# Runs of edges per target tile: ten partitions and three small matmuls in place of one partition, in a two-layer graph kernel

## The chip, the cores and the metric

The kernel runs on one core of one Trainium2 chip. The metric is the device time of one execution in microseconds, the median of three runs. A core has TensorE (matmuls and transposes into PSUM), VectorE, ScalarE, GpSimd, and SyncE, which issues most transfers. Each engine works through its own instructions in program order; engines are tied to each other only by semaphores.

## What is computed

Two graph attention networks with a layer norm behind each, on 1250 nodes of 768 features and 20000 edges sorted by target (self loops are added). The edges do not enter the kernel's later stages one by one: the first stage turns them into a matrix of counts C[dst, src], and the attention is then dense work on it. Of the reference, what the first stage needs:

```python
loops = jnp.arange(N)
src = jnp.concatenate([edge_index[0], loops])
dst = jnp.concatenate([edge_index[1], loops])
x1 = jax.nn.relu(x @ W_ah + b_ah)
# in every attention layer, per edge:
e = leaky_relu(as_n[src] + ad_n[dst], 0.2)
p = exp(e - segment_max(e, dst)[dst])
out = segment_sum(p / segment_sum(p, dst)[dst] * h[src], dst)
```

## The kernel before, in words

`gnn_two_layers` calls one stage after another (`counts_and_x1`, `project`, `aggregate_layer0` and so on). Each stage ends with a barrier of all engines, so a stage begins when the one before is over. The change lies in the first stage, `counts_and_x1`, alone.

**What the stage makes.** The counts of edges for ten tiles of 125 target nodes (T = 125, NT = 10), a mask from them, and x1 = relu(x W + b) transposed, for five blocks of 250 nodes (NB = 5). Products in float32 precision are made of a high and a low part of each operand (`w_hi`, `w_lo`, `xT_hi`, `xT_lo`).

**How edges are counted.** The 20000 edges lie on 40 partitions (ER = 40), 500 on each, and an edge run is one such partition; four steps (RUN = 4) of 125 edges make a run. VectorE casts them to float (L216) and takes least and greatest target of each run (L217, L218). TensorE turns edges and ends (L365, L368): the ends come out on all 128 partitions, 40 columns of least and 40 of greatest, in bank 1 of `p_turn`. Because edges are sorted, a target tile meets a contiguous range of runs. The kernel finds for every tile the first run, the number of runs and how many were handled before: `range_i[0, 0..2, tile]`. Before, VectorE does this on one partition with 10 x 40 = 400 elements (L222 to L241), in buffers that lie in the count matrix `CT`, and a scan makes the running sum. Every `step(...)` is an instruction that signals, and a wait for it (`Chain`).

**The loops over runs.** `one_hots(t)` on VectorE reads three values of `range_i` into registers and loops over the runs; for each of four steps it waits for a free buffer (`hot_free`), writes `src_hot` (125 x 1250, L254) and `dst_hot` (125 x 125, L255). `count(t)` on TensorE reads two values, opens the banks with three band matmuls (the self loops, L382) and adds `dst_hot` times `src_hot`, three matmuls a step (L388). Four buffers lie between the two.

**The order written out by hand.** VectorE: the ranges, `rest_of_x(0, 0)` (L269), then per block one_hots, two rest_of_x, score weights (L502), mask (L260), rest_of_x1, one_hots and so on. TensorE: turn the edges, wait for the constants and for `ranges_ready` (L373, L374), turn x (0, 0) and (0, 1) (L417), then per block count, turn_x, x1 products (L431), turn_row and so on. ScalarE rounds x (L322), stages the count rows (L309) and keeps turned rows. GpSimd: iotas and constants (L191 to L200), six tiles of W split into two parts (L204, L206; a copy `w_hi` and a difference `w_lo`), then the DMA issues of the score weights (L484, L488), each of which waits, from the fourth on, for VectorE's use. SyncE: edges, x, bias, then the six tiles of W, of which tile k waits until tile k - 2 is split (L182).

Of the kernel before, what the change touches and what calls it, by code (L numbers as in the profile page):

```python
# [101 lines left out]
def counts_and_x1(nc, core, src, dst, x, w_ah, b_ah, w_gat, a_gat):  # L102
# [4 lines left out]
    with ExitStack() as ctx:  # L107
        sb, pb, sem = core.tools(ctx)
        dst_ends = sb("dst_ends", [ER, 2], F32)
        ends_row = sb("ends_row", [128, 2, ER], F32)  # L110
        edge_col = sb("edge_col", [T, 2, RUN, 2 * ER], F32)

        spare = CT[0:1, :, :].rearrange("p t n -> p (t n)")[:, 0:2 * 5 * NT * ER].bitcast(F32) \
            .rearrange("p (a t e) -> p a t e", a=5, t=NT)
        meets, meets_b, meets_c = (spare[:, i] for i in range(3))
        tile_lo, run_no = (spare[:, i].bitcast(I32) for i in (3, 4))
        range_f = sb("range_f", [1, 3, NT], F32)
        ones_row = sb("ones_row", [1, NT], F32)
# [32 lines left out]
        ranges_ready = sem("ranges_ready")  # L151
        hot_ready = sem("hot_ready")
# [37 lines left out]
        def _(pool):  # L190
            pool.iota(node_no[:], [[1, N]], base=0, channel_multiplier=0).then_inc(consts, 1)  # L191
            pool.iota(tile_lo, [[T, NT], [0, ER]], base=0, channel_multiplier=0).then_inc(consts, 1)
            pool.iota(run_no, [[0, NT], [1, ER]], base=0, channel_multiplier=0).then_inc(consts, 1)
# [18 lines left out]
        def _(dve):  # L212
# [9 lines left out]
            step(v.tensor_copy(ends_row[:], p_turn[:, 1, 0:2 * ER].rearrange("p (a c) -> p a c", a=2)))  # L222
            dve.wait_ge(consts, 3)
            least = ends_row[0:1, 0:1, :].broadcast_to([1, NT, ER])
            most = ends_row[0:1, 1:2, :].broadcast_to([1, NT, ER])

            step(v.tensor_tensor(meets, most, tile_lo, ALU.is_ge))
            step(v.scalar_tensor_tensor(meets_b, tile_lo, float(T), least, ALU.add, ALU.is_gt))
            step(v.tensor_tensor(meets, meets, meets_b, ALU.mult))
            step(v.scalar_tensor_tensor(meets_b, run_no, float(-ER), meets, ALU.add, ALU.mult))  # L230
            step(v.scalar_tensor_tensor(meets_c, run_no, 1.0, meets, ALU.add, ALU.mult))
            step(v.tensor_reduce(out=range_f[:, 0, :], in_=meets_b, axis=AX.X, op=ALU.min))
            step(v.tensor_reduce(out=range_f[:, 1, :], in_=meets_c, axis=AX.X, op=ALU.max))
# [126 lines left out]
        def _(pe):  # L360
# [10 lines left out]
            nc.tensor.sem_inc(hot_free, RUN)  # L371
            nc.tensor.sem_inc(row_turned, 1)
            pe.wait_ge(consts, 8)  # L373
            pe.wait_ge(ranges_ready, 1)  # L374
            nc.tensor.sem_inc(ct_done, 1)

            def count(t):
# [1759 lines left out]
```

## Time and profile before

| | us |
|---|---|
| median of 3 runs | 2097.6 |
| lowest and highest | 2096.47, 2100.13 |
| the profiled execution | 2099.49 |
| its span, first to last instruction | 2097.7 |

| engine | busy us | share of the span | instructions |
|---|---|---|---|
| TensorE, matmuls | 1865.0 | 89% | 11272 |
| VectorE | 1492.5 | 71% | 2490 |
| ScalarE | 974.5 | 46% | 1463 |
| GpSimd | 166.1 | 8% | 139 |

TensorE's granted clock over the execution is 0.949 of full speed. The first stage ends near 262 us. In the rows, a time line gives the start in us, the duration in us (of several merged instructions, from the first to the last), the engine, line, operation, output and inputs by the program's names, shapes and count, and in square brackets the idle time in front of it and what ended it. DVE is VectorE, ACT ScalarE, POOL GpSimd, PE TensorE's matmuls, PEld its weight loads. Buffers that lie in others go by the outer one's name: `edge_i` is `x_f`, `edge_f` is `count_row`, `w_raw` is `G`. Durations on GpSimd are rough.

### The profile page before, as it was taken

The page shows a single profiled execution, that of the slowest core. Times are in us where ns is not written, and L with a number is a line of the kernel's source. Part 1 is how long each engine was busy: PE and PEld are TensorE (multiplying, and loading weights), DVE is VectorE, ACT ScalarE, POOL GpSimd, SP SyncE. Part 2 cuts the span into 40 slices and gives each one's busy share as a digit, 9 for nine tenths or more (in the row PEclk, how much of TensorE's full clock was granted, in tenths as well). Part 3 has the DMA queues.
Part 4 walks back from the last instruction along what each step waited for, and adds up shares of the span by engine and source line. Part 5 has one row for each costly group of instructions (what it writes and reads, how often), then busy time and mean ns, then how long its engine had stood idle before and what let it go on. Part 6 is the DMA issues. An engine that isn't in the chain of part 4 may idle for free. (4 is left out here: it accounts for less than half of the span.)

```text
span 2097.7 us, 29944 instructions
## 1 busy us (share of the span) xinstructions
PE 1865.0 (89%) x11272; PEld 1774.4 (85%) x11272; DVE 1492.5 (71%) x2490; ACT 974.5 (46%) x1463; POOL 166.1 (8%) x139
## 2 busy tenths in 40 slices
PE   5998899994999999994989889979999996999888
PEld 4666689994999999994989779978999995999888
DVE  7887759996888888862556619717888885235776
ACT  1222222215687897763222322217888885232433
POOL 5010022100000000000001012100000000000210
PEclk9999999996999999996999889989999998999999
DMA  3111154335243424307856445544423404644402
GB/s 115 49 53 49 38 157 147 104 87 137 65 130 95 108 87 123 89 13 219 236 138 184 137 149 151 169 129 131 143 82 106 139 34 132 176 108 131 116 1 74
DMA packets 203354, 237.69 MB, mean 113 GB/s; under 512 B 98741, under 2 KB 177677, under 8 KB 203224
## 3 DMA queue, kind: packets, MB, share of 16 engines
q1 hardware_dynamic: 195240, 208.32, 34.5%
q0 software_dynamic: 7216, 24.91, 4.0%
q10 hardware_dynamic: 768, 2.70, 0.4%
q8 instruction: 85, 1.39, 0.3%
q14 instruction: 45, 0.37, 0.1%
HBM read 173.99 MB, written 61.90 MB: 112 GB/s over the span
## 5 line engine op out<-in xcount | busy, mean ns | idle before, releaser
L946 PE MATMUL p_o<-h_in,p 125*125 125x193 f32 x2400 | 405.5, 332 | 41.5 <-DVE p L905 20.9
L946 PEld LDWEIGHTS p_o<-h_in,p 125*125 125x125 f32 x2400 | 399.3, 191 | 44.8 <-issue 23.7
L866 ACT ACTIVATE e<-uv,col 125x1250 f32<-125x1250 f32 x240 | 298.5, 1358 | 16.0 <-DMA uv<-uv_rows 14.9
L1404 PE MATMUL p_o<-p_hi,h_parts 125*128 125x416 f32 (+1 forms) x960 | 282.8, 355 | 24.7 <-DVE p_lo L1338 18.4
L1686 PE MATMUL p_y<-fw_hi,f_hi 128*125 128x384 f32 (+1 forms) x680 | 237.9, 350 | 60.7 <-DVE f_lo L1562 58.6
L1686 PE MATMUL p_y<-fw_lo,f_hi 128*125 128x384 f32 (+1 forms) x680 | 235.3, 346 | 0.0
L1686 PE MATMUL p_y<-fw_hi,f_lo 128*125 128x384 f32 (+1 forms) x680 | 234.6, 345 | 0.0
L1562 DVE TENSOR_TENSOR f_lo<-f_raw,f_hi 128x1125 fp32r<-128x1125 f32 (+1 forms) x80 | 101.1, 1265 | 173.6 <-ACT f_hi L1660 173.5
L900 DVE TENSOR_TENSOR e<-e 125x1250 f32<-125x1250 f32 x120 | 174.1, 1451 | 67.5 <-ACT e L866 67.4
L1404 PEld LDWEIGHTS p_o<-p_hi,h_parts 125*128 125x128 f32 x960 | 181.7, 189 | 30.8 <-issue 18.6
L1660 ACT ACTIVATE f_hi<-f_raw 128x1125 fp32r<-128x1125 f32 (+1 forms) x80 | 87.4, 1093 | 251.3 <-PE p_y L1686 215.3
L646 DVE CUSTOM_DVE_ANT_0 max_junk<-src_row,G 125x1250 bf16<-125x1250 f32 x120 | 180.9, 1581 | 9.3 <-DMA src_row<-score_rows 8.6
L733 PE MATMUL p_h<-pw_hi,x1T 128*125 128x384 f32 x720 | 186.2, 340 | 0.0
L1686 PEld LDWEIGHTS p_y<-fw_hi,f_hi 128*125 128x125 f32 x680 | 130.5, 192 | 64.9 <-issue 62.0
L905 DVE SCALAR_TENSOR_TENSOR p<-e,CT 125x1250 f32<-125x1250 f32 x120 | 175.3, 1461 | 5.7 <-PE p_o L946 1.7
L1146 PE MATMUL p_h<-pw_hi,x2T 128*125 128x256 f32 x960 | 173.7, 284 | 0.0
L1404 PE MATMUL p_o<-p_lo,h_parts 125*128 125x416 f32 (+1 forms) x480 | 169.9, 354 | 0.0
L1146 PEld LDWEIGHTS p_h<-pw_hi,x2T 128*125 128x125 f32 x960 | 148.4, 188 | 0.0
L388 PE MATMUL p_count<-src_hot,dst_hot 125*125 125x416 bf16 (+1 forms) x588 | 126.6, 372 | 18.9 <-DVE dst_hot L255 18.9
L1296 ACT ACTIVATE e<-uv,col 125x416 f32<-125x416 f32 (+1 forms) x240 | 139.6, 630 | 0.0
L1146 PE MATMUL p_h<-pw_lo,x2T 128*125 128x256 f32 x480 | 136.1, 284 | 0.0
L388 PEld LDWEIGHTS p_count<-src_hot,dst_hot 125*125 125x125 bf16 x588 | 73.8, 145 | 72.1 <-DVE dst_hot L255 55.4
(227 smaller groups left out, 3259.4 us busy)
## 6 DMA issues: line engine op xcount, KB each, us to landing
f_raw<-turned SPq DMA_DIRECT2D x40, 562.5 KB, 4.3
f_raw<-turned SPq DMA_DIRECT2D x40, 500.0 KB
h_rows<-h_out SPq DMA_DIRECT2D x32, 560.0 KB
h_parts<-h_rows SPq DMA_DIRECT2D x40, 448.0 KB
uv<-uv_rows SPq DMA_DIRECT2D x24, 546.9 KB
turned<-out_f SPq DMA_DIRECT2D x18, 625.0 KB
h_rows<-h_out SPq DMA_DIRECT2D x24, 424.4 KB
h_in<-h_rows SPq DMA_DIRECT2D x24, 424.4 KB
```

The source lines that it names most:

```text
L388: last = nc.tensor.matmul(p_count[:, i, 0:w], dst_hot[:, h, :], src_hot[:, h, a:a + w], start=False, stop=False, skip_group_check=True)
L646: v.tensor_tensor_reduce(out=junk[:, t % 2, :], in0=src_row[:, h % 2, :], in1=G[:, t, :], scale=1.0, scalar=NO_EDGE, op0=ALU.add, op1=ALU.max,
L733: last = nc.tensor.matmul(p_h[:, (u * NT + t) % 4, 0:width], xp[:, k, at], wp[:, u, k, :], start=(k == 0 and n == 0), stop=(k == KD - 1 an ...
L866: last = a.activation(e[:, g % RING, kind, :], uv[:, hh, kind, :], ACT.Exp, bias=col_src[kind][:, bass.ds(i * 2 + hh, 1), s])
L900: v.tensor_tensor(e[:, g % RING, 0, :], e[:, g % RING, 0, :], e[:, g % RING, 1, :], ALU.max).then_inc(more_ready, 1)
L905: v.scalar_tensor_tensor(p[:, g % RING, :], e[:, g % RING, 0, :], 1.0, CT[:, s, :], ALU.min, ALU.mult).then_inc(p_ready, 1)
L946: last = nc.tensor.matmul(p_o[:, b, n * 256:n * 256 + C0 + 1], p[:, g % RING, d * T:(d + 1) * T], h_in[:, hh, s, 0:C0 + 1], start=(s == 0 ...
L1146: last = nc.tensor.matmul(p_h[:, n % 4, 0:HALF1], xp[:, k, at], wp[:, q % 2, k, :], start=(k == 0 and j == 0), stop=(k == KD - 1 and j == 2))
L1296: last = a.activation(e[:, g % RING, kind, 0:w], uv[:, i % 2, kind, at:at + w], ACT.Exp, bias=col_src[kind][:, i, s:s + 1])
L1404: last = nc.tensor.matmul(p_o[:, bank(n, c), 0:w], h[:, s, kind, cols].bitcast(F32R), pp[:, g % RING, 0:w], start=(s == 0 and j == 0), sto ...
L1562: v.tensor_tensor(f_lo[:, kh], f_raw[:, kh], f_hi[:, kh].bitcast(F32), ALU.subtract).then_inc(f_lo_done, 1)
L1686: last = nc.tensor.matmul(p_y[:, t % 2, 0:CW + extra], fp[:, kh, kk, :], wp[:, k, :], start=(k == 0 and n == 0), stop=(k == K - 1 and n == 2))
```

## The change

The ranges are found with the ten tiles on ten partitions: each instruction then has 40 elements or one a partition, and the ends are read where TensorE put them, in PSUM, where every partition has them. The tile's first node comes from an iota over partitions. First run and count stand as two columns of `range_f` [10, 4]. TensorE brings them to one partition: two matmuls with the identity turn them, and one with `later` (1 where the column's tile is later than the row's) gives the sum of the counts of all tiles before, so the scan goes. VectorE casts the result from bank 2 of `p_turn` (L241's successor). GpSimd makes `later` with a memset, a wait and a select, ahead of its other constants. On TensorE the three matmuls stand behind a wait for `ranges_found`; the waits for the constants and for `ranges_ready` move behind `turn_x(0, 0)` and `turn_x(0, 1)`. Nothing else changes.

```diff
--- before.py
+++ after.py
@@ -107,15 +107,14 @@
     with ExitStack() as ctx:
         sb, pb, sem = core.tools(ctx)
         dst_ends = sb("dst_ends", [ER, 2], F32)
-        ends_row = sb("ends_row", [128, 2, ER], F32)
         edge_col = sb("edge_col", [T, 2, RUN, 2 * ER], F32)
 
-        spare = CT[0:1, :, :].rearrange("p t n -> p (t n)")[:, 0:2 * 5 * NT * ER].bitcast(F32) \
-            .rearrange("p (a t e) -> p a t e", a=5, t=NT)
-        meets, meets_b, meets_c = (spare[:, i] for i in range(3))
-        tile_lo, run_no = (spare[:, i].bitcast(I32) for i in (3, 4))
-        range_f = sb("range_f", [1, 3, NT], F32)
-        ones_row = sb("ones_row", [1, NT], F32)
+        tile_lo = sb("tile_lo", [NT, 2], F32)
+        tile_lo_i = sb("tile_lo_i", [NT, 1], I32)
+        run_no_i = sb("run_no_i", [NT, ER], I32)
+        meets = sb("meets", [NT, 3, ER], F32)
+        range_f = sb("range_f", [NT, 4], F32)
+        later = sb("later_tiles", [NT, NT], F32)
         range_i = sb("range_i", [1, 3, NT], I32)
         node_no = sb("node_no", [T, N], I16)
         src_hot = sb("src_hot", [T, RUN, N], BF16)
@@ -149,6 +148,9 @@
         edges_turned = sem("edges_turned")
         cols_ready = sem("cols_ready")
         ranges_ready = sem("ranges_ready")
+        later_ready = sem("later_ready")
+        ranges_found = sem("ranges_found")
+        ranges_turned = sem("ranges_turned")
         hot_ready = sem("hot_ready")
         hot_free = sem("hot_free")
         counted = sem("counted")
@@ -189,8 +191,12 @@
         @block.gpsimd
         def _(pool):
             pool.iota(node_no[:], [[1, N]], base=0, channel_multiplier=0).then_inc(consts, 1)
-            pool.iota(tile_lo, [[T, NT], [0, ER]], base=0, channel_multiplier=0).then_inc(consts, 1)
-            pool.iota(run_no, [[0, NT], [1, ER]], base=0, channel_multiplier=0).then_inc(consts, 1)
+            pool.iota(tile_lo_i[:], [[0, 1]], base=0, channel_multiplier=T).then_inc(consts, 1)
+            pool.iota(run_no_i[:], [[1, ER]], base=0, channel_multiplier=0).then_inc(consts, 1)
+            pool.memset(later[:], 1.0).then_inc(later_ready, 1)
+            pool.wait_ge(later_ready, 1)
+            pool.affine_select(out=later[:], in_=later[:], compare_op=ALU.is_gt, fill=0.0, base=0,
+                               pattern=[[1, NT]], channel_multiplier=-1).then_inc(later_ready, 1)
             for m in (band, ident_b, zeros_b):
                 pool.memset(m[:], 0.0).then_inc(consts, 1)
             pool.wait_ge(consts, 6)
@@ -219,26 +225,20 @@
             dve.wait_ge(edges_turned, 1)
             v.tensor_copy(edge_col[:, :, :, 0:ER],
                           p_turn[0:T, 0, 0:2 * RUN * ER].rearrange("p (a b c) -> p a b c", a=2, b=RUN)).then_inc(cols_ready, 1)
-            step(v.tensor_copy(ends_row[:], p_turn[:, 1, 0:2 * ER].rearrange("p (a c) -> p a c", a=2)))
             dve.wait_ge(consts, 3)
-            least = ends_row[0:1, 0:1, :].broadcast_to([1, NT, ER])
-            most = ends_row[0:1, 1:2, :].broadcast_to([1, NT, ER])
-
-            step(v.tensor_tensor(meets, most, tile_lo, ALU.is_ge))
-            step(v.scalar_tensor_tensor(meets_b, tile_lo, float(T), least, ALU.add, ALU.is_gt))
-            step(v.tensor_tensor(meets, meets, meets_b, ALU.mult))
-            step(v.scalar_tensor_tensor(meets_b, run_no, float(-ER), meets, ALU.add, ALU.mult))
-            step(v.scalar_tensor_tensor(meets_c, run_no, 1.0, meets, ALU.add, ALU.mult))
-            step(v.tensor_reduce(out=range_f[:, 0, :], in_=meets_b, axis=AX.X, op=ALU.min))
-            step(v.tensor_reduce(out=range_f[:, 1, :], in_=meets_c, axis=AX.X, op=ALU.max))
-            step(v.tensor_scalar(range_f[:, 0, :], range_f[:, 0, :], float(ER), float(ER - 1), ALU.add, ALU.min))
-            step(v.tensor_tensor(range_f[:, 1, :], range_f[:, 1, :], range_f[:, 0, :], ALU.subtract))
-            step(v.tensor_scalar(range_f[:, 1, :], range_f[:, 1, :], 1.0, None, ALU.max))
-            step(v.memset(ones_row[:], 1.0))
-
-            step(v.tensor_tensor_scan(range_f[:, 2, :], ones_row[:], range_f[:, 1, :], 0.0, ALU.mult, ALU.add))
-            step(v.tensor_tensor(range_f[:, 2, :], range_f[:, 2, :], range_f[:, 1, :], ALU.subtract))
-            v.tensor_copy(range_i[:], range_f[:]).then_inc(ranges_ready, 1)
+            step(v.tensor_copy(tile_lo[:, 0:1], tile_lo_i[:]))
+            step(v.tensor_scalar(tile_lo[:, 1:2], tile_lo[:, 0:1], float(T), None, ALU.add))
+            least, most = (p_turn[0:NT, 1, a * ER:(a + 1) * ER] for a in range(2))
+            step(v.tensor_scalar(meets[:, 0, :], most, tile_lo[:, 0:1], None, ALU.is_ge))
+            step(v.scalar_tensor_tensor(meets[:, 0, :], least, tile_lo[:, 1:2], meets[:, 0, :], ALU.is_lt, ALU.mult))
+            step(v.scalar_tensor_tensor(meets[:, 1, :], run_no_i[:], float(-ER), meets[:, 0, :], ALU.add, ALU.mult))
+            step(v.scalar_tensor_tensor(meets[:, 2, :], run_no_i[:], 1.0, meets[:, 0, :], ALU.add, ALU.mult))
+            step(v.tensor_reduce(out=range_f[:, 2:3], in_=meets[:, 1, :], axis=AX.X, op=ALU.min))
+            step(v.tensor_reduce(out=range_f[:, 3:4], in_=meets[:, 2, :], axis=AX.X, op=ALU.max))
+            step(v.tensor_scalar(range_f[:, 0:1], range_f[:, 2:3], float(ER), float(ER - 1), ALU.add, ALU.min))
+            v.tensor_scalar(range_f[:, 1:2], range_f[:, 3:4], range_f[:, 0:1], 1.0, ALU.subtract, ALU.max).then_inc(ranges_found, 1)
+            dve.wait_ge(ranges_turned, 1)
+            v.tensor_copy(range_i[:], p_turn[0:1, 2, 0:3 * NT].rearrange("p (a n) -> p a n", a=3)).then_inc(ranges_ready, 1)
             dve.wait_ge(ranges_ready, 1)
             dve.wait_ge(cols_ready, 1)
 
@@ -368,10 +368,13 @@
                 last = nc.tensor.transpose(p_turn[:, 1, a * ER:(a + 1) * ER],
                                            dst_ends[:, a:a + 1].broadcast_to([ER, 128]), ident[0:ER, 0:ER])
             last.then_inc(edges_turned, 1)
+            pe.wait_ge(later_ready, 2)
+            pe.wait_ge(ranges_found, 1)
+            for a in range(2):
+                nc.tensor.matmul(p_turn[0:1, 2, a * NT:(a + 1) * NT], range_f[:, a:a + 1], ident[0:NT, 0:NT], start=True, stop=True)
+            nc.tensor.matmul(p_turn[0:1, 2, 2 * NT:3 * NT], range_f[:, 1:2], later[:], start=True, stop=True).then_inc(ranges_turned, 1)
             nc.tensor.sem_inc(hot_free, RUN)
             nc.tensor.sem_inc(row_turned, 1)
-            pe.wait_ge(consts, 8)
-            pe.wait_ge(ranges_ready, 1)
             nc.tensor.sem_inc(ct_done, 1)
 
             def count(t):
@@ -437,6 +440,8 @@
 
             turn_x(0, 0)
             turn_x(0, 1)
+            pe.wait_ge(consts, 8)
+            pe.wait_ge(ranges_ready, 1)
             for b in range(NB):
                 count(2 * b)
                 turn_x(b, 2)
```

## Rows read from the trace of the kernel before

**Rows 1.** The page, part 1: engine, busy us, share of the span, instructions.
```profile
PE 1865.0 (89%) x11272; PEld 1774.4 (85%) x11272; DVE 1492.5 (71%) x2490; ACT 974.5 (46%) x1463; POOL 166.1 (8%) x139
```

**Rows 2.** Busy time of each engine by window of 10 us.
```profile
core 0: us, PE busy (x) PEld busy (x) DVE busy (x) ACT busy (x) POOL busy (x), PEclk, DMA share, GB/s
...
10.00:20.00 10.00, 0.00 (x0) 0.00 (x0) 9.72 (x10) 0.00 (x0) 9.50 (x7) 1.00 0.36 118
...
40.00:50.00 10.00, 9.19 (x76) 8.51 (x74) 6.61 (x31) 4.61 (x10) 2.15 (x4) 1.00 0.61 178
```

**Rows 3.** Timeline of VectorE, 9 to 42 us: start, duration, line.
```profile
9.87 0.49 DVE L220 COPY edge_col<-p_turn 125x320 f32<-125x320 f32 x1 [2.34 <-PE p_turn L368]
...
10.55 1.26 DVE L227 TENSOR_TENSOR CT<-ends_row,CT 1x400 f32<-1x400 f32 x1
...
12.95 1.80 DVE L229 TENSOR_TENSOR CT<-CT 1x400 f32<-1x400 f32 x1
...
18.32 0.56 DVE L233 TENSOR_REDUCE range_f<-CT 1x10 f32<-1x400 f32 x1
18.91 1.12 DVE L234 TENSOR_SCALAR range_f<-range_f 1x10 f32<-1x10 f32 x1
...
21.16 1.47 DVE L239 TENSOR_TENSOR_SCAN range_f<-ones_row,range_f 1x10 f32<-1x10 f32 x1
...
22.86 0.17 DVE L241 CAST range_i<-range_f 1x30 int32<-1x30 f32 x1
...
28.82 0.55 DVE L254 TENSOR_SCALAR src_hot<-node_no,edge_col 125x1250 bf16<-125x1250 int16 x1 [1.85 <-issue]
...
30.07 0.54 DVE L254 TENSOR_SCALAR src_hot<-node_no,edge_col 125x1250 bf16<-125x1250 int16 x1
...
39.22 0.67 DVE L269 TENSOR_TENSOR xT_lo<-p_x,xT_hi 128x500 fp32r<-128x500 f32 x1
...
41.85 0.35 DVE L502 CUSTOM_DVE_ANT_0 wa_by_junk<-wa_by_w,wa_by_a 128x192 bf16<-128x192 f32 x1
```

**Rows 4.** Timeline of GpSimd, 3 to 26 us.
```profile
3.10 0.48 POOL L193 IOTA CT<- 1x400 int32 x1
...
9.84 1.54 POOL L206 TENSOR_TENSOR w_lo<-G,w_hi 128x768 fp32r<-128x768 f32 x1
11.32 1.17 POOL L204 CAST w_hi<-G 128x768 fp32r<-128x768 f32 x1
12.57 1.75 POOL L206 TENSOR_TENSOR w_lo<-G,w_hi 128x768 fp32r<-128x768 f32 x1
14.58 0.86 POOL L204 CAST w_hi<-G 128x768 fp32r<-128x768 f32 x1 [0.26 <-DMA G<-in_w_ah]
...
18.46 1.54 POOL L206 TENSOR_TENSOR w_lo<-G,w_hi 128x768 fp32r<-128x768 f32 x1
...
23.86 1.54 POOL L206 TENSOR_TENSOR w_lo<-G,w_hi 128x768 fp32r<-128x768 f32 x1
25.34 0.71 POOL L484 DMA_DIRECT2D wa_by_a<-in_a_gat  x1
```

**Rows 5.** Timeline of TensorE and ScalarE at the first tiles of x.
```profile
23.13 1.90 PE L417 MATMUL p_x<-ident,x_in 125*128 125x125 f32 x8 [13.37 <-issue]
24.28 1.28 ACT L322 ACT_TABLE_LOAD   x1 [24.28 <-PE p_x L417]
```

**Rows 6.** Timeline near 92 us; landing times of line L488's 36 issues.
```profile
91.69 1.14 POOL L484 DMA_DIRECT2D wa_by_a<-in_a_gat  x1
91.90 0.81 DVE L260 TENSOR_SCALAR G<-count_row 125x1250 bf16<-125x1250 f32 x1
...
DMA to landing us min/median/max: 2.5/2.8/4.4
```

**Rows 7.** TensorE's groups, 29.5 to 32.9 us, then 33.2 to 39.3 us: busy, mean ns.
```profile
L388 PE MATMUL p_count<-src_hot,dst_hot 125*125 125x416 bf16 (+1 forms) x11 | 3.6, 510 | 3.5 <-DVE dst_hot L255 3.5
...
L388 PE MATMUL p_count<-src_hot,dst_hot 125*125 125x416 bf16 (+1 forms) x35 | 6.6, 344 | 0.0
```

## The prediction, made before the change was run

> **What bounds the kernel now.** The page first: TensorE is busy for 89% of the span [rows 1], and the chain that the page follows back from the last instruction stays in the last stage, so it says nothing of the first. What is done at the start is worth its time only if everything behind it moves up. So I read the windows of the first 30 us next: from 10 to 20 us TensorE does nothing while VectorE is busy for 9.72 and GpSimd for 9.50 of 10 us [rows 2]. Then the timeline by engine. VectorE's copy of the turned edges starts at 9.87, and a chain of fourteen small instructions follows, on one partition, each waiting for the one before, up to the cast at 22.86 to 23.03 [rows 3]. TensorE stands in front of `ranges_ready` and turns x only at 23.13 [rows 5]; ScalarE loads a table and rounds, VectorE forms the rest and reads three registers, and the first one-hot starts at 28.82 [rows 3, 5]. Every later step of the stage waits for counts, and counts wait for one-hots. No transfer with a time of its own stands behind this. So the quantity to forecast is **when the one-hots of tile 0 are through**: now at 39.22, where VectorE goes on to L269 [rows 3].
>
> **Why the chain takes 12.5 us.** The arithmetic is small, but its durations are not its own. L229 runs 12.95 to 14.75, and GpSimd's w_lo of 12.57 to 14.32 ends 0.43 before it; L239 (10 elements) runs 21.16 to 22.63 and L234 (10 elements) 18.91 to 20.03, GpSimd's instruction beside L234 ending at 20.00 [rows 3, 4]. L227 is held the same way to 11.38 and then needs 0.43. Not held: L233, a reduction that begins 0.14 before GpSimd's instruction of 18.46 and runs on beside it for 0.42 us, and L220, which reads PSUM and lies wholly beside GpSimd's w_lo of 9.84 to 11.38 [rows 3, 4]. So VectorE's SBUF-to-SBUF forms and GpSimd's instructions exclude each other. They alternate: at 11.38 VectorE, which had waited, went first, and GpSimd's cast of 11.32 took 1.17 in place of 0.86 [rows 4].
>
> **GpSimd's side of it.** It splits six tiles of W, 0.86 and 1.54 us each, with gaps for the loads (0.26 before 14.58), and ends at 25.40; then come its four DMA issues [rows 4]. The change hardly touches this: two iotas of 400 elements (0.48 each) go; two small iotas, a memset, an own wait and a 10x10 select come. Small ones step by about 0.1, the wait and the select by 0.3 each, in all about 0.9 against 0.96, so at most 0.3 either way. That passes to GpSimd's end and to the result at up to one for one. The load of tile k starts when tile k-2 is split, so GpSimd's end is held near 25 by its own work and the round trips of its loads, whether VectorE is quick or not.
>
> **Part by part: the ranges.** Removed: L222 (0.2) and all of L227 to L240. Added on VectorE, after the copy that ends at 10.36: ten small instructions and a cast, and between them three matmuls. My walk, with GpSimd's instructions at 0.86 and 1.54 where they are not held:
> - tile_lo's cast and the add of T read and write SBUF. One element a partition is not in the trace; from below each costs 0.15 (a free small instruction), from above it is held as L234 was. I take held, because L234 is the nearest row: to 11.42, then behind GpSimd's cast to 12.25.
> - Two comparisons that read PSUM: free as L220, 0.2 each, to 12.7.
> - Two products with both inputs in SBUF, 40 elements: the first is held by w_lo to about 13.95, the second falls in GpSimd's wait for its load, 14.1.
> - Two reductions as L233 but with 40 elements, to 14.45; two more small instructions on [10,1], the last behind GpSimd's cast of 14.58, to 15.45.
> So `ranges_found` comes at 15.5; at 13.1 if one-element instructions are never held. TensorE's three matmuls and the semaphores: eight transposes took 1.90 [rows 5], 0.24 each, so 0.7, and x is turned from 16.2. VectorE's cast of the turned ranges lies beside that.
>
> **The x tiles.** The transposes of x wait for nothing that the ranges give, but in program order they stand behind the three matmuls, so the move hides only the last cast. From TensorE's first transpose of x to the first one-hot it is 5.69 now (23.13 to 28.82: transposes, table, rounding, rest, register reads [rows 3, 5]) and nothing in it changes. First one-hot: 16.2 + 5.7 = **21.9**, 6.9 us earlier. With 13.1 it is 19.5.
>
> **What is late next.** At 21.9 GpSimd still has the rest of one w_lo, a cast and a w_lo to do. Now the one-hots start 3.4 us after GpSimd is through and never meet it; no row shows L254 beside a GpSimd computation. It runs SBUF to SBUF with one tensor input, as L234 does, so I take it as held: first one-hot behind the w_lo of 20.85 (to 22.4), done 22.9; its small partner behind the cast, 23.9; the second behind the last w_lo (to 25.45), its partner done at 26.05. Then fourteen steps are left. A step is 0.62 (two from 28.82 to 30.07), sixteen of them took 10.40 (28.82 to 39.22), that is 9.9 and 0.5 in which TensorE, slow at first, held the ring of four buffers. End: 26.05 + 14 x 0.62 + 0.5 = 35.2, against 39.22: **4.0 us**. From 19.5 the same walk gets three steps through before GpSimd ends and gives 34.7, 4.5 us. So about 5 of the gained microseconds meet GpSimd's, and what is saved hardly depends on how long the range chain gets. The 0.5 for the slow TensorE may be spent already beside GpSimd, which lifts 4.0 to 4.5 too. I take **4.3**.
>
> **The DMA issues behind it.** GpSimd's four issues for the score weights, now at 25.34 to 27.64 on an idle VectorE, come under full one-hots. L484 at 91.69 took 1.14 where it took 0.71 at 25.34, and ended 0.12 after L260, beside which it lay [rows 4, 6]. So an issue waits for one VectorE instruction: four of at most 1.2 us end by 30.5, and with 4.4 to landing, the longest [rows 6], the weights are there at 35; L502 wants them at about 37.8 (now 41.85, and 4.0 less [rows 3]). Covered, with 2.8 us to spare; without it each microsecond is lost. The Trainium skill (SBUF — State Buffer, "A bandwidth-pool intuition that's wrong") states a harsher case: a software-generated DMA of about 620 ns took 3100 ns beside a VectorE copy. By that, four issues would end at about 38 and the weights land at 42; no row of this case shows more than the 1.14.
>
> **The sum.** 4.3 us off everything behind it, as the stages follow each other by barriers. The profiled execution's 2099.49 (span 2097.7) becomes 2095.2; it lies 1.9 above the median 2097.6, from which I forecast 2093.3.
>
> **Rivals.**
> - *No exclusion for one-hots* (10%): the whole gain stays, 6.9 (21.9 + 10.4 = 32.3) to 9.3 us with the shorter chain: 2088.3 to 2090.7. For it: nothing but the missing row. Against: L234.
> - *GpSimd is starved* (12%): back-to-back one-hots don't let it in. They end at 32.3, the last split at 35.3, the second DMA issue at 36.5 lands at 40.9, and L502 starts there in place of 41.85: 1 us saved, 2096.6. Against: at 11.38 the one that waited went before the back-to-back one. The skill's figure above would give the same time.
> - *The chain isn't short* (5%): all eight small steps that are no reductions are held, by 1.3 each (the mean of GpSimd's cast and w_lo, with a gap). Then it comes at 20.8, the first one-hot at 27.2, the end at 37.6: 1.6 us saved, 2096.0. The change then fails to do what it says.
> - *Slower, through TensorE's clock* (5%): in the 3.4 us after 29.5 the count's matmuls took 510 ns on the mean, later 344 [rows 7], with TensorE 13 us idle not long before. Fed with a step each 1.6 us beside GpSimd, it may stay at 1.2 GHz until the count is over. Eleven matmuls took 3.6 us, so a step of three costs 0.98, and fourteen from 26.05 end at 39.8: 0.6 late. If the level holds on through the x1 products (76 matmuls in 9.2 us at the high one [rows 2]) up to 8 us more are lost: 2098.2 to 2106, 2102 in the middle. It decides from the point where the level rises only after 33 us.
>
> **How the numbers follow.** My case has 68% and gives 2092 to 2094.8 with the median's own scatter of a microsecond; it is 2093.3. The range: 2089.8 to 2096.8 takes in the starved and the long chain and part of the first rival, and leaves out its lower end and the slow one. A measurement can tell about 0.2%, 4.2 us, from no change, and my forecast lies on that line: half of my case (34%) and the first rival are faster by more, with a part for unknowns 47%; the other half and the two small gains make 47% within; slower 6%.
>
> **What would show it.** In the changed profile: ranges cast done at 14 to 17 us; the first one-hot at 19.5 to 22.5; L254 instances of 1 us and more while GpSimd splits, and GpSimd's w_lo of 1.9 to 2.1; the last w_lo ending at 25 to 26.5; GpSimd's DMA issues at 0.6 to 1.2; L502 not waiting for them; and L269 of group 1 near 35. One-hots of 0.55 beside GpSimd's work would make the first rival true; a wait of L502 for wa_by_w the second. I am wrong by more than 2 us if a later stage has a wait that gives the time back, or if TensorE's granted clock, 0.949 on the mean, shifts by a thousandth or two.

## The result, and the profile after

The changed kernel takes 2089.24 us (median of 7 runs, 2084.95 to 2095.25) against 2098.65 for the kernel before (7 runs, 2092.54 to 2101.0): a ratio of 0.9963, 95% interval 0.9946 to 0.9981. It is faster, by 4 to 11 us. The forecast was 2093.3, in a range of 2089.8 to 2096.8, made on a median of 2097.6 for the kernel before; by the ratio that is 2089.8 (0.9963 x 2097.6), at the very edge of the range (the median itself, 2089.24, lies 0.6 below it), and the direction was right. Two executions, of 6058 and 7938 us, both of the kernel before, are left out of every mean and median below. The profiled execution took 2089.24, its span is 2087.5.

The chain of ranges on VectorE, whose counterpart is [rows 3] (start, duration, line, operation, output and inputs, shapes):

```profile
9.84 0.49 DVE L226 COPY edge_col<-p_turn 125x320 f32<-125x320 f32 x1 [2.35 <-PE p_turn L368]
10.25 0.13 DVE L229 CAST tile_lo<-tile_lo_i 10x1 f32<-10x1 int32 x1
10.41 0.14 DVE L230 TENSOR_SCALAR tile_lo<-tile_lo 10x1 f32<-10x1 f32 x1
...
11.16 0.84 DVE L234 SCALAR_TENSOR_TENSOR meets<-run_no_i,meets 10x40 f32<-10x40 int32 x1
12.03 0.19 DVE L235 SCALAR_TENSOR_TENSOR meets<-run_no_i,meets 10x40 f32<-10x40 int32 x1
...
12.86 0.20 DVE L239 TENSOR_SCALAR range_f<-range_f 10x1 f32<-10x1 f32 x1
13.54 0.18 DVE L241 CAST range_i<-p_turn 1x30 int32<-1x30 f32 x1 [0.48 <-PE p_turn L375]
```

The ranges are ready at 13.72 in place of 23.03. Of the ten small instructions one is held, L234, until GpSimd's cast of 11.12 is over. The one-hots that follow, on the same engine:

```profile
19.34 0.55 DVE L254 TENSOR_SCALAR src_hot<-node_no,edge_col 125x1250 bf16<-125x1250 int16 x1 [1.82 <-issue]
19.81 0.25 DVE L255 TENSOR_SCALAR dst_hot<-node_no,edge_col 125x125 bf16<-125x125 int16 x1
19.97 1.17 DVE L254 TENSOR_SCALAR src_hot<-node_no,edge_col 125x1250 bf16<-125x1250 int16 x1
21.06 1.53 DVE L255 TENSOR_SCALAR dst_hot<-node_no,edge_col 125x125 bf16<-125x125 int16 x1
22.51 1.14 DVE L254 TENSOR_SCALAR src_hot<-node_no,edge_col 125x1250 bf16<-125x1250 int16 x1
23.57 1.53 DVE L255 TENSOR_SCALAR dst_hot<-node_no,edge_col 125x125 bf16<-125x125 int16 x1
25.02 0.53 DVE L254 TENSOR_SCALAR src_hot<-node_no,edge_col 125x1250 bf16<-125x1250 int16 x1
...
34.32 0.67 DVE L269 TENSOR_TENSOR xT_lo<-p_x,xT_hi 128x500 fp32r<-128x500 f32 x1
```

And GpSimd beside them, whose counterpart is [rows 4]:

```profile
17.66 1.55 POOL L212 TENSOR_TENSOR w_lo<-G,w_hi 128x768 fp32r<-128x768 f32 x1
19.98 0.82 POOL L210 CAST w_hi<-G 128x768 fp32r<-128x768 f32 x1 [0.77 <-DMA G<-in_w_ah]
20.88 1.66 POOL L212 TENSOR_TENSOR w_lo<-G,w_hi 128x768 fp32r<-128x768 f32 x1
22.48 0.82 POOL L210 CAST w_hi<-G 128x768 fp32r<-128x768 f32 x1
23.39 1.66 POOL L212 TENSOR_TENSOR w_lo<-G,w_hi 128x768 fp32r<-128x768 f32 x1
24.99 0.71 POOL L489 DMA_DIRECT2D wa_by_a<-in_a_gat  x1
```

The first one-hot starts 9.5 us earlier (19.34 for 28.82), but `dst_hot`, a quarter of a microsecond by itself, takes 1.53 twice: each time GpSimd's w_lo began 0.18 before it, and it ends 0.05 after that w_lo. From 19.97 to 25.02 two steps get done where eight would have. Tile 0's one-hots are through at 34.32 in place of 39.22: of 9.5 us, 4.9 arrive. From 25.02, when GpSimd is done with W, every instruction has its plain length again; what then still stretches some steps is the ring of four buffers, while TensorE is slow.

The remaining 4.3 us of the shorter first stage came after tile 0, in code that the change doesn't touch. Of the windows below, the first two are of before, the third of the changed kernel (after the busy times stand the granted clock, the share of DMA and GB/s):

```profile
190.00:200.00 10.00, 6.70 (x23) 4.30 (x23) 8.18 (x27) 0.91 (x3) 0.55 (x1) 0.66 0.07 22
40.00:250.00 210.00, 193.39 (x1194) 142.12 (x1193) 170.70 (x646) 48.72 (x106) 21.07 (x37) 0.96 0.19 55
```

```profile
40.00:250.00 210.00, 195.27 (x1225) 141.32 (x1224) 173.87 (x664) 49.97 (x109) 20.70 (x37) 0.98 0.18 52
```

TensorE ran 17 of these 210 us at 1.2 GHz before (the rest at 2.4, so 0.96 on the mean) and about 7 in the changed kernel. Whether that belongs to the change is what half of the experiments are for.

### The profile page after: what moved, and what is told of

Same layout as the page of the kernel before. It is cut to its first block and busy times, and to the rows that moved or that the text cites. A ratio compares the mean times of both kernels' runs of the same rounds, so it can differ in the third digit from the quotient of the medians.

```text
span 2087.5 us, 29956 instructions
## 1 busy us (share of the span) xinstructions
PE 1864.0 (89%) x11278; PEld 1770.0 (85%) x11278; DVE 1485.9 (71%) x2486; ACT 974.5 (47%) x1463; POOL 163.4 (8%) x141
## 5 line engine op out<-in xcount | busy, mean ns | idle before, releaser
L651 DVE CUSTOM_DVE_ANT_0 max_junk<-src_row,G 125x1250 bf16<-125x1250 f32 x120 | 185.8, 1617 | 9.3 <-DMA src_row<-score_rows 8.7
L391 PE MATMUL p_count<-src_hot,dst_hot 125*125 125x416 bf16 (+1 forms) x588 | 126.3, 368 | 19.5 <-DVE dst_hot L255 19.5
```

The source lines that it names most:

```text
L391: last = nc.tensor.matmul(p_count[:, i, 0:w], dst_hot[:, h, :], src_hot[:, h, a:a + w], start=False, stop=False, skip_group_check=True)
L651: v.tensor_tensor_reduce(out=junk[:, t % 2, :], in0=src_row[:, h % 2, :], in1=G[:, t, :], scale=1.0, scalar=NO_EDGE, op0=ALU.add, op1=ALU.max,
```

## The experiments

Theory A is that of the prediction: VectorE's SBUF-to-SBUF instructions and GpSimd's exclude each other, so GpSimd's splitting of W, over at 25, is a floor under the first tile. Theory B, the rival, has dependences alone. For the gain behind tile 0: by P the half-clock stretches fall by chance, the same for both kernels; by Q something steady in the kernels makes the difference.

All kernels, from their profiles. "Rest" is the time from tile 0's last one-hot to the next stage's first memset; the clock is the mean of the window 40 to 250 us. The last columns are the median time and the ratio to the kernel before.

The runs were made in four batches, the last three on three different chips, and each batch has its own runs of the kernel before: median 2098.65 with the result; 2100.14 with move only, ranges only, slow ranges and GpSimd late; 2098.67 with changed again, six slots and the first pair with zeros; 2096.66 with before again, x first and the freed pair. A ratio compares within its batch. Medians of different batches don't compare to better than these 3 us.

| kernel | first one-hot | GpSimd done with W | tile 0's one-hots through | rest | clock | median | ratio, 95% interval |
|---|---|---|---|---|---|---|---|
| before | 28.82 | 25.40 | 39.22 | 223.4 | 0.96 | 2098.65 | |
| before, again | 28.73 | 25.67 | 40.08 | 221.9 | 0.97 | 2098.18 | 1.0005, 0.9993 to 1.0016 |
| changed | 19.34 | 25.05 | 34.32 | 219.1 | 0.98 | 2089.24 | 0.9963, 0.9946 to 0.9981 |
| changed, again | 19.21 | 25.46 | 33.87 | 222.2 | 0.97 | 2089.30 | 0.9950, 0.9937 to 0.9963 |
| move only | 25.42 | 25.48 | 35.71 | 223.3 | 0.96 | 2095.45 | 0.9979, 0.9969 to 0.9989 |
| ranges only | 19.44 | 25.08 | 33.62 | 219.1 | 0.98 | 2089.95 | 0.9943, 0.9927 to 0.9960 |
| slow ranges | 22.20 | 24.55 | 35.08 | 220.0 | 0.98 | 2093.55 | 0.9976, 0.9962 to 0.9990 |
| GpSimd late | 18.99 | 35.34 | 30.35 | 224.3 | 0.98 | 2092.53 | 0.9969, 0.9953 to 0.9986 |
| six slots | 19.21 | 23.66 | 32.99 | 221.5 | 0.97 | 2091.62 | 0.9954, 0.9938 to 0.9969 |
| x first | 16.29 | 25.91 | 32.69 | 219.5 | 0.98 | 2088.54 | 0.9964, 0.9949 to 0.9980 |
| zeros, before | 28.66 | 25.61 | 38.57 | 219.5 | 0.99 | 2095.58 | 0.9977, 0.9964 to 0.9991 |
| zeros, changed | 19.30 | 24.98 | 33.82 | 219.2 | 0.99 | 2087.06 | 0.9942, 0.9929 to 0.9955 |
| freed | 15.61 | 21.00 | 31.19 | 219.8 | 0.98 | 2091.14 | 0.9969, 0.9956 to 0.9983 |
| freed, zeros | 16.93 | 20.58 | 29.67 | 219.5 | 0.99 | 2086.56 | 0.9947, 0.9927 to 0.9967 |

### The move alone

```diff
-            pe.wait_ge(consts, 8)
-            pe.wait_ge(ranges_ready, 1)
             nc.tensor.sem_inc(ct_done, 1)
...
             turn_x(0, 1)
+            pe.wait_ge(consts, 8)
+            pe.wait_ge(ranges_ready, 1)
```

> The kernel before, with only the waits for the constants and for ranges_ready moved behind the first two turns of x; the ranges are still found on one partition. Theory A (VectorE's SBUF-to-SBUF instructions and GpSimd's exclude each other, and GpSimd's splits of W until about 25.4 us are a floor): the range chain ends at 23.0 as before, the transposes, the table and the rounding are over by then, so the first one-hot starts at about 25.6 in place of 28.82, just behind GpSimd, and tile 0's one-hots are through at 36.0 in place of 39.22: 3.2 us, two thirds of the changed kernel's 4.9 from moving two lines. Theory B (the chain of dependences alone counts, no exclusion): the same 3.2 here, but then the short range chain would be worth 6.3 more. Both: total time 3.2 us less than before.

As expected: first one-hot at 25.42, through at 35.71. Two moved lines of the old kernel are worth 3.5 us, without a faster range chain.

### The ranges alone

The changed kernel, with the two waits put back ahead of `turn_x(0, 0)`.

> The changed kernel with the waits put back in front of the first turns of x: the new ranges alone. The three matmuls precede the turns in either order, and VectorE's cast of the ranges takes 0.2, so both theories: first one-hot 19.3 to 19.6 (19.34 with the move), one-hots of tile 0 through at 34.3 to 34.5. The move is worth under 0.3 us beside the new ranges.

The first one-hot came at 19.44, so beside the new ranges the move is worth 0.1 us. The end, 33.62, was 0.7 below that of the first profile of the changed kernel and 0.25 below that of the second; how far such ends scatter is shown below, where the same kernels run again.

### A slower chain

```diff
             step(v.tensor_scalar(range_f[:, 0:1], range_f[:, 2:3], float(ER), float(ER - 1), ALU.add, ALU.min))
+            for _ in range(14):
+                step(v.tensor_reduce(out=meets[:, 1, 0:1], in_=most, axis=AX.X, op=ALU.max))
```

> The changed kernel with 14 idle reductions that read PSUM (0.22 us each, not held by GpSimd) put into the range chain: ranges_found comes 3.1 us later and the first one-hot at 22.4 in place of 19.34. Theory A: the delay falls into time in which GpSimd keeps the one-hots back anyway; tile 0's one-hots are through at 34.9 to 35.2 in place of 34.32, so 0.6 to 0.9 of the 3.1 us arrive. Theory B: all 3.1 arrive, 37.4.

VectorE's timeline:

```profile
12.61 3.06 DVE L240 TENSOR_REDUCE meets<-p_turn 10x1 f32<-10x40 f32 x14
...
22.20 0.95 DVE L256 TENSOR_SCALAR src_hot<-node_no,edge_col 125x1250 bf16<-125x1250 int16 x1 [1.83 <-issue]
23.07 1.53 DVE L257 TENSOR_SCALAR dst_hot<-node_no,edge_col 125x125 bf16<-125x125 int16 x1
24.52 0.54 DVE L256 TENSOR_SCALAR src_hot<-node_no,edge_col 125x1250 bf16<-125x1250 int16 x1
...
35.08 0.67 DVE L271 TENSOR_TENSOR xT_lo<-p_x,xT_hi 128x500 fp32r<-128x500 f32 x1
```

The first one-hot is 2.9 us later, the last 0.8 (against 34.32; 1.2 against the 33.87 of the second profile). The delay went into GpSimd's time. Theory B wanted 37.4 and falls. This is shown for tile 0 alone: by the medians (2093.55, and 2089.95 for "ranges only" in the same batch, 10 and 4 runs with standard deviations of 4) the whole 3 us could have arrived.

### GpSimd's last two tiles late

```diff
             for k in range(KD):
+                if k == 4:
+                    pool.wait_ge(hot_ready, 16)
```

> The changed kernel with GpSimd's last two tiles of W split only after the sixteen one-hot steps of tile 0 (a wait on hot_ready in front of tile 4). Theory A: no one-hot is longer than 0.56, the first still starts at 19.3, and they are through at 29.8 to 30.2 in place of 34.32; but the same 4.7 us of GpSimd's work then stand in front of the x1 products, which start at about 35 (35.51 in the changed kernel), and the score weights' transfers, issued at 35 and landed near 39.5, hold VectorE for about 2 us more: the time is 1 to 3 us above the changed kernel. Theory B: one-hots already through at the chain's pace, so the end at 34.3 would not move.

```profile
18.99 0.55 DVE L256 TENSOR_SCALAR src_hot<-node_no,edge_col 125x1250 bf16<-125x1250 int16 x1 [1.82 <-issue]
19.45 0.25 DVE L257 TENSOR_SCALAR dst_hot<-node_no,edge_col 125x125 bf16<-125x125 int16 x1
19.61 0.54 DVE L256 TENSOR_SCALAR src_hot<-node_no,edge_col 125x1250 bf16<-125x1250 int16 x1
...
23.30 0.55 DVE L256 TENSOR_SCALAR src_hot<-node_no,edge_col 125x1250 bf16<-125x1250 int16 x1 [0.33 <-PE p_count L393]
...
30.35 0.67 DVE L271 TENSOR_TENSOR xT_lo<-p_x,xT_hi 128x500 fp32r<-128x500 f32 x1
...
40.29 0.36 DVE L509 CUSTOM_DVE_ANT_0 wa_by_junk<-wa_by_w,wa_by_a 128x192 bf16<-128x192 f32 x1 [7.24 <-DMA wa_by_w<-in_w_gat]
```

With GpSimd away no one-hot is held, and they are through 4.0 us earlier than in the changed kernel, of which 0.35 are an earlier first one-hot. The end is 0.15 later than I had expected, since TensorE's slow matmuls held the ring. The other 3.6 are the price of the exclusion, measured by itself. But the work only moved: the splits end at 35.34, the score weights' transfers are issued behind them, and VectorE waits 7.2 us; L509 starts at 40.29 where its counterpart in the changed kernel started at 37.01. I had put 2 us on that wait, it cost 3.3. Three runs (median 2092.53, ratio 0.9969) don't tell the total from the changed kernel's.

### Room for six raw tiles of W

`w_raw` gets six slots in the same buffer, SyncE's wait for the splits goes, and each tile has a semaphore of its own.

> The changed kernel with room for all six raw tiles of W, so that no load waits for a split. Theory A (GpSimd's splits are the floor): GpSimd no longer waits for loads (0.4, 0.7 and 0.8 us now) and ends near 23.5 in place of 25.05; the first one-hot stays at 19.3 and tile 0's one-hots are through at 33.2 to 33.6 in place of 34.3, without a change to VectorE's chain. Theory B (only the chain counts): 34.3 as before. Total 0.7 to 1.2 us less than the changed kernel, which so many runs can hardly tell.

GpSimd no longer waits for loads and is done at 23.66, 1.4 us sooner; the chain and the first one-hot (19.21) stand where they were; the one-hots are through at 32.99, 0.9 to 1.3 sooner and just ahead of what I had expected. A stall of GpSimd, an engine busy for 8% of the span, was on the path. The median, 2091.6 (the changed kernel's in the same batch is 2089.3), doesn't show it: one microsecond is below what these runs resolve.

### x first

The two turns of x go ahead of the wait for `ranges_found` too.

> The changed kernel with the first two turns of x ahead of the wait for ranges_found as well. Transposes, table and rounding are over when the ranges come, so the first one-hot starts near 16.2 in place of 19.3. Theory A (GpSimd's floor near 25): one or one and a half more steps get through between GpSimd's instructions, and tile 0's one-hots end at 32.9 to 33.5 in place of 33.9 to 34.3: 3 us earlier at the start, under 1 at the end. Theory B: 31.0.

The start came as expected, 16.29, and the end at 32.69, just past my interval. VectorE's timeline shows that more steps slip through than I thought, and GpSimd's timeline says why:

```profile
16.29 0.85 DVE L254 TENSOR_SCALAR src_hot<-node_no,edge_col 125x1250 bf16<-125x1250 int16 x1 [1.85 <-issue]
17.06 0.81 DVE L255 TENSOR_SCALAR dst_hot<-node_no,edge_col 125x125 bf16<-125x125 int16 x1
17.79 0.53 DVE L254 TENSOR_SCALAR src_hot<-node_no,edge_col 125x1250 bf16<-125x1250 int16 x1
18.25 1.53 DVE L255 TENSOR_SCALAR dst_hot<-node_no,edge_col 125x125 bf16<-125x125 int16 x1
```

```profile
16.75 1.08 POOL L210 CAST w_hi<-G 128x768 fp32r<-128x768 f32 x1
17.90 1.82 POOL L212 TENSOR_TENSOR w_lo<-G,w_hi 128x768 fp32r<-128x768 f32 x1
19.87 1.04 POOL L210 CAST w_hi<-G 128x768 fp32r<-128x768 f32 x1
20.99 1.82 POOL L212 TENSOR_TENSOR w_lo<-G,w_hi 128x768 fp32r<-128x768 f32 x1
```

Here a held `dst_hot` and a free `src_hot` get through between two instructions of GpSimd, where in the changed kernel only one did: two steps for each tile of W in place of one. GpSimd pays with longer instructions (1.82 for 1.54, 1.04 for 0.82), not with waits for loads, of which it has none of more than 0.15 us from 16.75 on. The starts of `src_hot` and of the cast beside it lie close (19.70 and 19.87 here, 22.51 and 22.48 in the changed kernel); what decides who goes first is not shown. So 3.0 us at the start gave 1.2 to 1.6 at the end. The floor is not rigid, and it can be pushed: GpSimd was done at 25.91.

### The same kernels again

> The changed kernel once more, to see what repeats. In five profiles so far the first stage from the end of tile 0's one-hots to the next stage's first memset took 223.4 us (before), 219.1 (changed), 223.3, 219.1 and 220.0, with 17.1 us of half clock inside it in the long ones and 7 to 10 in the others. Theory P: those half-clock stretches fall by the phase of the clock's own grid, which differs from run to run, and no part of the change is behind them; then tile 0's one-hots end at 34.3 again within 0.7, the rest takes anything between 218 and 224, and the gain of the total over many runs tends to about 5 us. Theory Q: the changed kernel has something steady that shortens the rest by 4; then the rest is 219 again and the total stays 8 to 9 us below before.

> The kernel before once more, for a second profile of it. Over all nine profiles so far the rest of the first stage is close to 216.4 us plus 0.41 us for each us of half clock in it (6.8 gives 219.1, 13.7 gives 222.2, 17.1 gives 223.4). Theory P (the phase of the clock's grid decides): tile 0's one-hots through at 38.5 to 39.3, the rest between 218 and 224 by that same line. Theory Q (something steady in the old kernel's rest): 223.3 to 223.5 for the third time, with 17.1 us of half clock.

The rest of the stage is no fixed property of either kernel. The changed one took 222.2 where it had taken 219.1; the old one 221.9 where it had taken 223.4. It goes with the clock column in every row but one: 223.3 and 223.4 at 0.96, 221.5 to 222.2 at 0.97, 219.1 to 220.0 at 0.98. (The exception is GpSimd late, whose rest holds the 7.2 us wait.) Q as a steady 223.4 falls. A leaning does not: the three profiles with the old ranges have a rest of 222.9 on the mean, the six with the new ones (changed twice, ranges only, slow ranges, six slots, x first) 220.2, and chance alone gives such a difference rarely. Whether the change makes the stretches fewer stays open.

TensorE's slow matmuls show inside tile 0 too, in the second profile of the kernel before:

```profile
33.04 0.55 DVE L254 TENSOR_SCALAR src_hot<-node_no,edge_col 125x1250 bf16<-125x1250 int16 x1 [0.33 <-PE p_count L388]
33.50 0.25 DVE L255 TENSOR_SCALAR dst_hot<-node_no,edge_col 125x125 bf16<-125x125 int16 x1
34.08 0.55 DVE L254 TENSOR_SCALAR src_hot<-node_no,edge_col 125x1250 bf16<-125x1250 int16 x1 [0.33 <-PE p_count L388]
```

TensorE's matmuls took 0.48 us on the mean from 31 to 36 us and 0.34 behind, VectorE waits for a free buffer, and a step takes 1.04 instead of 0.62. (The clock column reads 1.00 here all the same. In the first profile of the changed kernel it reads 0.50 from 19.9 to 30.2, with matmuls of 0.53 and then 0.34 and the same steps of 1.04: in tile 0 the matmuls tell the level better than the column.) Here the sixteen steps took 11.35 us and lost 1.4 to that, in the first profile 0.5. So ends differ by up to 0.9 us between profiles of the same kernel. In the pair of the changed kernel it is the other cause: four steps got done before GpSimd was through with W in the second profile, three in the first, and in "ranges only" three by 25.05 and a shorter loss to the ring.

The total of the changed kernel, however, came out at 9.4 below again. Over all runs of both, the mean is 2098.05 for the kernel before (79 runs, standard error 0.33) and 2090.1 for the changed one (12 runs, 0.85): 8.0 us, plus or minus 1.8. Within the two batches that have both it is 7.5 and 9.6, together 8.6, plus or minus 2.2. The first tile accounts for 5.6 (39.65 and 34.10 on the mean of two profiles each). A fit with one slope for the time at half clock, over all kernels' runs, gives 7.1 at equal clock. So some 1.5 to 3 us are not accounted for by tile 0, about as much as the error, and as much as the leaning of the rest.

The total scatters more than the first stage does. From the next stage's first memset to the end of the span the two profiles of the kernel before took 1835.1 and 1840.9 us, those of the changed kernel 1834.1 and 1831.6, "ranges only" 1840.7: 9.3 us between the lowest and the highest of the fourteen profiles, in code that is the same in all. The two profiles of the kernel before end the first stage within 0.6 us of each other and differ by 5.2 in their span. The granted clock behind the first stage is 0.95 and 0.94 in them, so it goes the same way; that it is the whole cause is not shown.

### TensorE kept busy in its waits

```diff
+                for _ in range(0 if t % 2 else 10 if t else 8):
+                    nc.tensor.matmul(p_count[:, 2, 0:416], zeros_b[:], band[:, 0:416], start=False, stop=False, skip_group_check=True)
                 with pe.Fori(0, count_) as j:
```

> The kernel before, with ten matmuls of zeros (eight at tile 0) added to the count's banks behind the band at every even tile, where TensorE waits 2.0 to 3.5 us for the first one-hot; the counts don't change. Theory P (half-clock stretches follow these waits): one-hots of tile 0 end at 39.2 as before, but the half-clock stretches between 60 and 250 us are gone or down to one, and the rest of the stage takes 216 to 219 in place of 223.4, so the total is 4 to 7 us less than before. If the stretches have nothing to do with these waits, the total is that of before or up to 2 us more.

> The changed kernel with the same matmuls of zeros. Theory P: with the stretches gone in both, only the first tile differs, so this is 4.9 us (4 to 6) faster than the kernel before with the zeros, and 0 to 4 us faster than the changed kernel. Theory Q: 8 to 9 us faster than the kernel before with the zeros.

What a stretch costs is read from the length of a count. In the kernel before, without the zeros, the 60 matmuls of tile 3 took 12.47 us. Tile 4 had one stretch, tile 7 a double one:

```profile
120.20 13.08 PE L388 MATMUL p_count<-src_hot,dst_hot 125*125 125x418 bf16 x60 [2.05 <-DVE dst_hot L255]
...
194.02 14.09 PE L388 MATMUL p_count<-src_hot,dst_hot 125*125 125x418 bf16 x60 [3.30 <-DVE dst_hot L255]
```

That is 0.6 and 1.6 us more. The windows, the kernel before with the zeros and the changed one with them:

```profile
40.00:250.00 210.00, 201.07 (x1258) 144.51 (x1257) 174.14 (x672) 50.02 (x109) 21.61 (x38) 0.99 0.19 55
```

```profile
40.00:250.00 210.00, 201.58 (x1264) 145.09 (x1264) 173.01 (x660) 50.12 (x110) 20.53 (x36) 0.99 0.18 51
```

In both the clock is at 0.99, one half-clock stretch is left, and the rest of the stage is 219.5 and 219.2: equal to 0.3 us, where the first profiles of the unaided kernels differed by 4.3 (the second ones by 0.3 the other way). That is a little above the 216 to 219 that I had expected. Tile 0's sixteen steps in the kernel before took 9.9 us, so with the zeros the ring lost nothing there. The gain over the first tile is 4.75. On the means of their runs the two differ by 6.8 (2094.3, 9 runs, and 2087.5, 5 runs; standard error 1.4), between what P and Q wanted. With 48 matmuls more, the old kernel gets 4.6 us faster on the mean (by the ratio 2 to 8).

### A version that frees GpSimd

Six slots, x first, and ScalarE rounds W; GpSimd makes only the differences. The last kernel adds the zeros to it.

```diff
+            def round_w(k):
+                act.wait_ge(w_in[k], 16)
+                nc.scalar.activation(w_hi[:, k, :], w_raw[:, k, :], ACT.Copy).then_inc(w_rounded, 1)
+            round_w(0)
+            round_w(1)
             round_x(0, 0)
             round_x(0, 1)
+            for k in range(2, KD):
+                round_w(k)
...
             for k in range(KD):
-                pool.wait_ge(w_in[k % 2], 16 * (k // 2 + 1))
-                pool.tensor_copy(w_hi[:, k, :], w_raw[:, k % 2, :]).then_inc(w_split, 1)
-                pool.wait_ge(w_split, 2 * k + 1)
+                pool.wait_ge(w_rounded, k + 1)
```

> A version meant to be faster: x first, six raw slots for W, and ScalarE, idle until 15 us, makes the rounded half of W, so that GpSimd has only the six differences (1.55 us each). GpSimd ends at 19.5 to 20.5 in place of 25.05, the first one-hot starts near 16.3. Theory A: the one-hots of tile 0 are through at 29.5 to 30.3, 4 us before the changed kernel, and the total is 2085 to 2087, 4 us below it. Theory B: the same start 16.3 gives 26.7 to 27.7.

> The same version with the matmuls of zeros at even tiles. From the pair with and without them (2094.3 against 2098.9 on the kernel before, 2087.5 against 2089.3 on the changed one, means): the rest of the stage at about 219 us whatever the phase, one-hots through at 29.5 to 30.3, total 2082 to 2085.

ScalarE and GpSimd in the freed version:

```profile
9.25 1.28 ACT L341 ACT_TABLE_LOAD   x1 [9.25 <-DMA G<-in_w_ah]
10.55 1.58 ACT L341 ACTIVATE w_hi<-G 128x768 fp32r<-128x768 f32 x2
...
11.47 9.53 POOL L208 TENSOR_TENSOR w_lo<-G,w_hi 128x768 fp32r<-128x768 f32 x6 [3.10 <-ACT w_hi L341]
```

GpSimd starts its first difference 1.8 us later than it did (11.47 for 9.64), because ScalarE loads its table first; it is done at 21.00, not 20. And TensorE's slow matmuls (0.53 to 0.56 us on the mean from 21 to 27 us) held the ring: the last fourteen steps took 10.2 us in place of 8.7. So 31.19 in place of 30; with the zeros, 29.67. The time of the freed version, 2091.14, is above the 2085 to 2087 that I had expected, and by its ratio (0.9969) it is not below the changed kernel (0.9963 and 0.9950): 2.7 to 3.1 us won in tile 0 do not show. With the zeros it is 2086.56, above the 2082 to 2085 expected; the changed kernel with them has 2087.06. Both are faster than the kernel before (ratios 0.9947 and 0.9942). That they are faster than the changed kernel without zeros is not shown, since the intervals overlap, and which of the two is better is open.

## Why the prediction was right, and where not

**What bounds tile 0, and the exclusion.** Right, and shown: the one-hots were held by GpSimd as forecast ("I take it as held"), down to the taking of turns and to w_lo growing from 1.54 to 1.66 (forecast 1.9 to 2.1, too much; in the other profiles the longest took 1.87). That they take turns one for one is no rule: in "x first" two of VectorE's got through to one of GpSimd's.

**The ranges.** Here a term was mis-sized. I took the two one-element instructions as held, "because L234 is the nearest row"; L229 and L230 took 0.13 and 0.14 beside a w_lo of 9.64 to 11.18, and L239 was free too. `ranges_found` came at 13.06, not 15.5, which was my other bound (13.1), and the first one-hot at 19.34, not 21.9 (bound: 19.5). Of the signs named beforehand, two were missed by this: the cast was done at 13.72, not at 14 to 17, and the first one-hot started just ahead of 19.5. It cost the forecast little, for the reason that the prediction gave: what is saved hardly depends on the length of the chain. That sentence is well supported, by "slow ranges".

**The end of tile 0.** Forecast 35.2, or 34.7 with the short chain; measured 34.32 and 33.87. The 4.3 us of the sum were 4.9 in the pair of profiles and 5.6 on the mean of two pairs. Two terms were off and nearly cancel in the changed kernel, which is luck: VectorE was free of GpSimd at 25.02, where my walk had 26.1, and the thirteen steps left took 9.3 us, that is 1.2 for TensorE's slow matmuls where I had 0.5. In the kernel before that loss was 0.5 in one profile and 1.4 in the other, and this, with the changed kernel's 33.87, lifts the mean gain.

**The DMA issues.** Covered, as forecast: three issues took 1.88 in place of 1.60, L507 starts at 37.01 with no wait for them. The harsher case of the Trainium skill (SBUF — State Buffer, "A bandwidth-pool intuition that's wrong") did not occur here: the trace has 0.63 us an issue under full one-hots. "GpSimd late" shows what a late issue costs.

**The total.** 4.3 forecast, 9.4 measured by medians, 7.8 by the ratio and 8.0 by means. The direction and the mechanism of tile 0 were right; the size was not. Two steps failed. One is "with the median's own scatter of a microsecond": single runs scatter with standard deviations of 1.2 to 4.1 us. The three runs of before that I had lay within 4 us, and I read that as the whole. The other is that everything behind tile 0 was taken to move up unchanged. In the first pair of profiles the rest of the first stage was 4.3 us shorter, with 7 us of half clock in place of 17, and in the fourteen profiles the later stages took anything within 9.3 us. The prediction had named the clock, "shifts by a thousandth or two", as its way to be off by 2 us, without a price; by the fit over all runs a thousandth is worth 1.3 us, and at equal clock 7.1 of the 8.0 us stay. That leaves tile 0's 5.6 against the 4.3 of the sum, and 1.5 us or more whose cause is open. The range held only just.

**The rivals.** No exclusion: out, by 1.53 us for `dst_hot`. Starved GpSimd: out, the one most held was longer by 0.12 in the first profile and 0.35 in the second. The long chain: out, `ranges_found` came at 13.06. TensorE's clock: it did stay low, but was high again at 30.2, and the rival began at 33. One sum in the prediction is off: half of its case, the starved and the long chain make 51% within 4.2 us of no change, where it has 47%; nothing else hangs on it.

## What to carry to other kernels

Before a chain of small VectorE instructions is shortened, lay GpSimd's timeline beside it: where durations end with GpSimd's instructions, part of the chain is waiting, and what follows will meet the same wait. Ask then when GpSimd is done and what its own waits are; a ring of two slots for its input was worth 0.9 to 1.3 us to VectorE. Where times of single runs differ by more than the effect, compare a milestone in the profile, and trust the total only over many runs of one batch.

## What the runs showed of the hardware that I had not expected

- SBUF-to-SBUF instructions with one element a partition were not held by GpSimd (0.13, 0.14 and 0.20 us beside it), while one with ten elements (L234, 1.12 us) was [rows 3]. The Trainium skill (Vector Engine (DVE) Microarchitecture Reference, "5.1 Performance modes — why throughput varies by op and dtype") gives as the condition for the mode that uses both ports that the outermost dimension other than one is even, or odd and equal in input and output. One element has no such dimension, and the page doesn't say what holds then; the trace shows no holding.
- TensorE's granted clock fell within 1.6 us of the start of a count in front of which TensorE had waited 1.8 us or more, in some profiles and not in others (0.66 in the window 190 to 200 us of the kernel before, 1.00 in the changed one); each such stretch held VectorE's ring (1.04 us a step for 0.62). Filling the waits of the five even tiles with 48 matmuls of zeros kept the clock at 0.99 and made the old kernel 4.6 us faster on the mean.
